# A fused graph-convolution and state-space kernel: row scaling moved behind the matmul, steps respaced over the units

## The reference, cut to what matters

```python
X = layernorm(x)
e = leaky_relu(sj[:, None, :] + si[:, :, None] + ab, 0.2)     # sj, si: X times folded vectors
alpha = adj * exp(e)
transition = alpha / (sum(alpha, -1, keepdims=True) + 1e-12)
H, Xk = 0, X
for k in range(3):
    H = H + Xk @ Wk[k] + bk[k]
    Xk = transition @ Xk
x = x + relu(H)                                               # x1
h = layernorm(x) @ W_fc1.T + b_fc1                            # then the state-space block:
u, z = split(h @ W_in.T);  u = silu(conv4(u) + conv_b)        # 1024 channels each
dt, B, C = split(u @ W_xproj.T)
delta = softplus(dt @ W_dt.T + b_dt)
s_t = exp(delta_t * A) * s_(t-1) + delta_t * u_t * B_t        # 16 states for each channel
y_t = sum over states of s_t * C_t
out = x + ((y + u * D) * silu(z)) @ W_out.T @ W_fc2.T + b_fc2
```

## Time and profile before

| | us |
|---|---|
| median of 3 runs | 4050.89 |
| lowest, highest | 4047.82, 4072.03 |
| the profiled execution | 4070.29 |
| its span, first to last instruction | 4068.2 |
| mean granted TensorE clock | 0.970 of full speed |

### The profile page before, as it was taken

How to read it: one execution, slowest core, us unless ns; L and a number is a source line. 1 busy time by engine, 2 the same in 40 slices (tenths; PEclk the granted TensorE clock), 3 DMA queues, 4 the chain that set the end, 5 groups by cost and what they waited for, 6 DMA issues and landing times. The chain is left out here.

```text
span 4068.2 us, 43314 instructions
## 1 busy us (share of the span) xinstructions
PE 3525.4 (87%) x10938; PEld 1962.4 (48%) x10938; DVE 3650.5 (90%) x3133; ACT 2835.8 (70%) x6002; POOL 3452.9 (85%) x1860
## 2 busy tenths in 40 slices
PE   6888888888888888888888888888888888888887
PEld 3544545444554444554444554444545444545443
DVE  0499999999999999999999999999999999999898
ACT  1477766777677777677777677777676777777765
POOL 0298888998888998888998888998888998888899
PEclk9889999999999999999999999999999999999999
DMA  2111101111101111101111101111101111101110
GB/s 103 49 51 54 54 11 45 51 53 53 54 8 49 51 54 53 53 9 48 51 53 53 54 7 50 51 54 53 53 11 45 51 53 53 54 11 42 47 47 8
DMA packets 50714, 183.77 MB, mean 45 GB/s; under 512 B 7339, under 2 KB 33203, under 8 KB 42067
## 3 DMA queue, kind: packets, MB, share of 16 engines
q1 hardware_dynamic: 48880, 174.17, 11.1%
q10 hardware_dynamic: 1636, 7.83, 0.5%
HBM read 164.15 MB, written 17.83 MB: 45 GB/s over the span
## 5 line engine op out<-in xcount | busy, mean ns | idle before, releaser
L408 POOL TENSOR_TENSOR st<-st,bc 128x1024 f32<-128x1024 f32 x1024 | 2400.9, 2361 | 429.1 <-DVE st L842 428.6
L842 DVE TENSOR_TENSOR_SCAN st<-dec,st 128x1024 f32<-128x1024 f32 x1024 | 2310.7, 2274 | 16.8 <-ACT dec L461 12.9
L667 PE MATMUL y_ps<-st,ident 128*128 128x512 f32 x4096 | 2010.9, 620 | 253.3 <-POOL st L408 253.3
L461 ACT ACTIVATE dec<-delta,decay 128x254 f32<-128x254 f32 x4096 | 1694.3, 467 | 612.1 <-DVE st L842 609.1
L667 PEld LDWEIGHTS y_ps<-st,ident 128*128 128x128 f32 x4096 | 770.3, 196 | 1067.8 <-issue 587.9
L830 DVE TENSOR_TENSOR st<-du,bc 128x1024 f32<-128x1024 f32 x736 | 882.1, 1199 | 5.3 <-ACT du L447 4.7
L399 POOL TENSOR_TENSOR st<-du_sb,bc 128x1024 f32<-128x1024 f32 x288 | 680.1, 2361 | 0.1
L868 DVE SCALAR_TENSOR_TENSOR u<-d_ps,chan,u 128x250 f32<-128x250 f32 (+2 forms) x768 | 307.8, 469 | 108.0 <-ACT u L501 107.3
L663 PE MATMUL y_ps<-u,diag 128*128 128x256 f32 x512 | 160.7, 441 | 229.6 <-DVE zs L849 229.6
L717 PE MATMUL d_ps<-xnT,wxz 128*128 128x256 f32 x1024 | 247.7, 385 | 6.6 <-ACT zs L510 6.6
L705 PE MATMUL d_ps<-xnT,wxz 128*128 128x256 f32 x1024 | 247.0, 384 | 6.2 <-DVE u L868 4.9
(11 more groups left out here) (99 smaller groups left out, 2527.4 us busy)
## 6 DMA issues: line engine op xcount, KB each, us to landing
bc<-bc_dram SPq DMA_DIRECT2D x64, 2048.0 KB, 10.2
xg<-x_dram SPq DMA_DIRECT2D x32, 256.0 KB, 11.5
x_dram<-xg SPq DMA_DIRECT2D x32, 256.0 KB, 2.0
last_x<-x_dram SPq DMA_DIRECT2D x32, 256.0 KB, 2.6
out_dram<-last_x SPq DMA_DIRECT2D x32, 256.0 KB, 2.2
bc<-w_inT_dram ACTq DMA_DIRECT2D x1, 4096.0 KB
adjt<-adjT_dram SPq DMA_DIRECT2D x32, 128.0 KB, 11.2
bc<-w_out_dram ACTq DMA_DIRECT2D x1, 2048.0 KB
```

What stands on the lines that cost most here:

```text
L408: nc.gpsimd.tensor_tensor(st[:, sl, :, :, :], st[:, sl, :, :, :], bc[:, p, 1, SU * q:SU * q + SU, None, :].to_broadcast([P, SU, 2, T]), AL ...
L461: a = nc.scalar.activation(dec[:, v % 2, s, j, :].rearrange("p (b t) -> p b t", b=PAIR)[:, :, 1:], delta[:, p, 2 * i + j, :].rearrange("p ...
L667: mm = nc.tensor.matmul(y_all, ident[:, :], st[:, sl, s, :, :].rearrange("p j t -> p (j t)"), start=False, stop=(q == Q - 1 and s == SU - ...
L842: nc.vector.tensor_tensor_scan(h, dec[:, v % 2, :, :, :].rearrange("p s j t -> p (s j t)"), h, 0.0, ALU.mult, ALU.add).then_inc(S["scanned ...
```

## The change

It has two parts.

First, the attention is no longer divided by its row sums before it is used. The row sum becomes two matmuls with a column of ones, which give a column per sequence (`g0[:, b:b+1]`); epsilon and reciprocal work on 128x2 (`rowsum`, `rinv`). The matmul with `att` comes first and spreads undivided values into the bank ("spread", with `x2k` in phase 18 and `x1k` in 22); ScalarE scales the two halves of the bank in place by `rinv` (phases 19 and 23); then the product with `Wk` is accumulated onto it (`hop`, phases 20 and 24, 25), without opening the bank anew.

Second, steps are respaced: u's projections to units 0, 3, 6, 9 with the taps two units behind, Silu of u 10 to 14, edge 8 to 12, Silu of z 3 to 6, the projection to dt, B, C to 15 and 16, dt to 18, 20, 22, 24, Exp to 22 and 26, Ln to 27; the graph's phases `xT` 8 to 7, third hop 9 to 8, `x2k` 11 to 9, e 12 to 10, exponentials 14 to 12, max 15 to 13, row sum 17 to 15, `x1k` 24 to 21, x1 28 to 27. z's units stay, and so do GpSimd's.

```diff
-U_STEPS = (0, 2, 4, 6)
+U_STEPS = (0, 3, 6, 9)
 Z_STEPS = (26, 27, 28, 29)
-X_STEPS = (12, 13)
-DT_STEPS = (15, 17, 19, 21)
-EXP_STEPS = (19, 23)
-LN_STEP = 24
-SILU_U, SILU_Z = 10, 3
+X_STEPS = (15, 16)
+DT_STEPS = (18, 20, 22, 24)
+EXP_STEPS = (22, 26)
+LN_STEP = 27
+SILU_U, SILU_Z = 14, 6
-FOLD_OUT = (1, 3, 5, 7)
-EDGE_STEP = 8
+FOLD_OUT = (1, 4, 7, 10)
+EDGE_STEP = 12
...
 ScalarE, graph_act
-                if v == 8:
+                if v == 7:
                     wait(act, "transposed", 2 * g + 1)
...
-                if v == 11:
+                if v == 9:
                     wait(act, "x2k_mm", g + 1)
...
-                if v == 14:
+                if v == 12:
                     wait(act, "e_mm", g + 1)
...
-                if v == 24:
+                if v in (19, 23):
+                    n = int(v == 23)
+                    wait(act, "rinv_made", g + 1)
+                    wait(act, "spread", 2 * g + 1 + n)
+                    for b in range(PAIR):
+                        half = g0[:, b * DIM:(b + 1) * DIM]
+                        a = nc.scalar.activation(half, half, ACT.Copy, scale=rinv[:, b:b + 1])
+                    a.then_inc(S["spread_scaled"], 1)
+                if v == 21:
                     wait(act, "x1k_mm", g + 1)
                     nc.scalar.activation(x1k[:, :, :].rearrange("p b d -> p (b d)"), g0[:, :], ACT.Copy)\
...
 TensorE, graph_pe
-                if v == 17:
+                if v == 15:
                     wait(pe, "alpha_made", g + 1)
-                    nc.tensor.matmul(g0[:, 0:T], ones[:, :], att[:, :, :].rearrange("p b i -> p (b i)"),
-                                     start=True, stop=True).then_inc(S["rowsum_mm"], 1)
-                if v in (21, 22):
-                    b = v - 21
-                    wait(pe, "att_made", g + 1)
-                    hop(b, 1, True, False)
-                    mm = nc.tensor.matmul(g0[:, b * DIM:(b + 1) * DIM], att[:, b, :], x2k[:, b, :],
-                                          start=False, stop=True, skip_group_check=True)
...
+                    for b in range(PAIR):
+                        mm = nc.tensor.matmul(g0[:, b:b + 1], att[:, b, :], one_col[:, 0:1], start=True, stop=True)
+                    mm.then_inc(S["rowsum_mm"], 1)
+                if v in (18, 22):
+                    if v == 18:
+                        wait(pe, "rinv_made", g + 1)
+                    else:
+                        wait(pe, "x1k_made", g + 1)
+                    for b in range(PAIR):
+                        mm = nc.tensor.matmul(g0[:, b * DIM:(b + 1) * DIM], att[:, b, :], (x2k if v == 18 else x1k)[:, b, :],
+                                              start=(b == 0), stop=False, skip_group_check=True)
+                    mm.then_inc(S["spread"], 1)
+                if v == 20:
+                    wait(pe, "spread_scaled", 2 * g + 1)
+                    for b in range(PAIR):
+                        mm = hop(b, 1, False)
+                    mm.then_inc(S["x1k_mm"], 1)
+                if v in (24, 25):
+                    b = v - 24
                     if b == 0:
-                        nc.tensor.matmul(g0[:, :], ones3, bk_row, start=True, stop=False, skip_group_check=True)
-                    hop(b, 0, False, False)
-                    mm = nc.tensor.matmul(g0[:, b * DIM:(b + 1) * DIM], att[:, b, :], x1k[:, b, :],
-                                          start=False, stop=(b == PAIR - 1), skip_group_check=True)
+                        wait(pe, "spread_scaled", 2 * g + 2)
+                        nc.tensor.matmul(g0[:, :], ones3, bk_row, start=False, stop=False, skip_group_check=True)
+                    mm = hop(b, 0, False)
...
 VectorE, conv and graph_dve
-                        if v == start + 1:
+                        if v == start + 2:
                             tap(dve, g, r, i, n)
...
-                if (v, late) == (15, 1):
+                if (v, late) == (13, 1):
                     wait(dve, "e_exp", g + 1)
...
-                if (v, late) == (19, 0):
+                if (v, late) == (16, 1):
                     wait(dve, "rowsum_mm", g + 1)
-                    nc.vector.tensor_scalar(g0[:, 0:T], g0[:, 0:T], EPS_ROW, None, ALU.add)\
+                    nc.vector.tensor_scalar(rowsum[:, :], g0[:, 0:PAIR], EPS_ROW, None, ALU.add)\
                         .then_inc(S["rowsum_eps"], 1)
                     wait(dve, "rowsum_eps", g + 1)
-                    nc.vector.reciprocal(g0[:, T:2 * T], g0[:, 0:T]).then_inc(S["rinv_made"], 1)
-                    wait(dve, "rinv_made", g + 1)
-                    nc.vector.tensor_tensor(att[:, :, :].rearrange("p b i -> p (b i)"), g0[:, T:2 * T],
-                                            att[:, :, :].rearrange("p b i -> p (b i)"), ALU.mult)\
-                        .then_inc(S["att_made"], 1)
-                if (v, late) == (28, 0):
+                    nc.vector.reciprocal(rinv[:, :], rowsum[:, :]).then_inc(S["rinv_made"], 1)
+                if (v, late) == (27, 0):
                     wait(dve, "h_mm", g + 1)
```

More of the change, by code:

```diff
@@ L124, in build @@
         x2k = sb("x2k", [P, PAIR, DIM])
-        ones = sb("ones", [P, P])
+        one_col = sb("one_col", [P, 1])
+        rinv = sb("rinv", [P, PAIR])
+        rowsum = sb("rowsum", [P, PAIR])
         last_x = sb("last_x", [P, PAIR, DIM])
@@ L176, in build @@
         dec_zeroed diag_made x_loaded adj_loaded stats aggr veps_made rstd_pow rstd_made normed transposed xT_made xnT_made
-        x2k_mm x2k_made e_mm e_exp alpha_max alpha_made rowsum_mm rowsum_eps rinv_made att_made x1k_mm x1k_made
+        x2k_mm x2k_made e_mm e_exp alpha_max alpha_made rowsum_mm rowsum_eps rinv_made spread spread_scaled x1k_mm x1k_made
         h_mm x1_made x1_stored x1_reloaded
@@ L754, in graph_pe @@
                     mm.then_inc(S["transposed"], 1)
-                if v == 9:
+                if v == 8:
                     wait(pe, "xT_made", g + 1)
                     for b in range(PAIR):
-                        mm = hop(b, 2, True, True)
+                        mm = hop(b, 2, True)
                     mm.then_inc(S["x2k_mm"], 1)
-                if v == 12:
+                if v == 10:
                     wait(pe, "x2k_made", g + 1)
@@ L771, in graph_pe @@
                     mm.then_inc(S["e_mm"], 1)
-                if v == 17:
+                if v == 15:
                     wait(pe, "alpha_made", g + 1)
-                    nc.tensor.matmul(g0[:, 0:T], ones[:, :], att[:, :, :].rearrange("p b i -> p (b i)"),
-                                     start=True, stop=True).then_inc(S["rowsum_mm"], 1)
-                if v in (21, 22):
-                    b = v - 21
-                    wait(pe, "att_made", g + 1)
-                    hop(b, 1, True, False)
-                    mm = nc.tensor.matmul(g0[:, b * DIM:(b + 1) * DIM], att[:, b, :], x2k[:, b, :],
-                                          start=False, stop=True, skip_group_check=True)
-                    if b == 1:
-                        mm.then_inc(S["x1k_mm"], 1)
@@ L786, in graph_pe @@
-                if v in (25, 26):
-                    b = v - 25
-                    wait(pe, "x1k_made", g + 1)
+                    for b in range(PAIR):
[10 more added lines that the diff above has]
+                    mm.then_inc(S["spread"], 1)
@@ L795, in graph_pe, with hop @@
                     if b == 1:
                         mm.then_inc(S["h_mm"], 1)
-            def hop(b, n, opens, closes):
+            def hop(b, n, opens):
                 for c in range(KC):
                     mm = nc.tensor.matmul(g0[:, b * DIM:(b + 1) * DIM], xT[:, c, b * L:(b + 1) * L], wks[:, n, c, :],
-                                          start=(opens and c == 0), stop=(closes and c == KC - 1),
+                                          start=(opens and c == 0), stop=(b == PAIR - 1 and c == KC - 1),
@@ L814, in _ @@
         def _(dve):
-            nc.vector.memset(ones[:, :], 1.0)
+            nc.vector.memset(one_col[:, :], 1.0)
             nc.vector.memset(ones3, 1.0)
```

## The result

The changed kernel takes 4167.48 us (median of 4 runs, 4155.02 to 4181.52) against 4053.95 of the kernel before beside it: a ratio of 1.027, 95% interval 1.0225 to 1.0322. The profiled execution took 4181.5 us, 14 us above the median.

What follows compares the result with a forecast made beforehand. VectorE, 90% busy and nearly without gaps, was taken as the bound. New waits 10.75, old waits -7.59, work -2.23, small gaps -0.4 made +0.5 us per iteration, +14 over 29: 4065 us by the median, range 3985 to 4120.

Steps and rivals of the forecast that it cites:

- VectorE's work: On VectorE, 256-column epsilon, reciprocal and multiply (2.61 us) give way to two small operations (0.38): 2.23 us saved per iteration.
- Silu's wait: Silu of u moved from unit 10 to 14, with the copy of `du`, makes scan 16 wait 1.85 us.
- Ln's: Ln moved from unit 24 to 27, behind z's first projection and bias, makes scan 29 wait 2.7 us.
- It stands in for the 1.62 at the gate of unit 18: The new 1.85 us at scan 16 replaces the old 1.62 us wait at the gate of unit 18.
- The wait at the iteration's end: `x1k`, last in ScalarE's iteration, waits for the hops: scan 0 waits 3.9 us and scan 31 0.5, plus two additions.
- loop end: ScalarE's 2.04 us standstill at the loop body's end, once in two iterations, is exposed behind `x1k`: 0.95 us per iteration.
- lower clock: TensorE, idle about 3 us before z2, runs slower, about 1.7 us in half of the iterations: 0.85 us.
- The waits that go: VectorE's old waits at taps, gate of unit 18, max and row sum could all go: 7.59 us per iteration.
- (a): Rival, chance 0.13: no new wait at scan 0, since TensorE reaches the hops before ScalarE gets to `x1k`; 3900 us.
- (b): Rival, chance 0.12: Ln is hidden in unit 27 while the other waits come; 3987 us.
- (c): Rival, chance 0.13: TensorE runs at half clock before z2 in every iteration; 4090 us.
- (d): Rival, chance 0.20: ScalarE gets stuck in units 19 to 25, scan 21 waits 1.8 us; 4117 us.

Runs made afterwards that it cites:

- the graph part alone: Attention and its hops as in the changed kernel, dense steps where the kernel before had them: 4140.87 us, 1.021 against the kernel before.

## Why the prediction was wrong

The forecast was 4065, and slower by over 1% had 0.26, for another reason. Per iteration it had +0.5; the traces say 125.9 - 122.0 = +3.9, a miss of 3.4. Added up over the same 28 iterations, VectorE's waits are 14.4 us each in the changed kernel, where 10.75 were reckoned, and 8.0 in the kernel before, where 7.59 were taken.

- **VectorE's work**: -2.23 reckoned. From the epsilon to the next inject the two small operations now take 2040.88 - 2040.63 = 0.25, so -2.36. Right (VectorE in the changed kernel):

```profile
2040.63 0.13 DVE L947 TENSOR_SCALAR rowsum<-g 128x2 f32<-128x2 f32 x1
2040.80 0.17 DVE L950 RECIPROCAL rinv<-rowsum 128x2 f32<-128x2 f32 x1
2040.88 1.22 DVE L847 TENSOR_TENSOR st<-du,bc 128x1024 f32<-128x1024 f32 x1
```

- **Silu's wait**: 1.85 at scan 16; measured 1.84. **Ln's**: 2.7 at scan 29; measured 2.72 and 2.73. Right, with their causes.
- **"It stands in for the 1.62 at the gate of unit 18"**: this is the step that failed. The gate waits 2.76 beside Silu's 1.84, not in its place; summed over the 29 rows of the timeline that stand in unit 18 it is some 78 us, 2.7 per iteration: most of the miss, by a wait that the sum had at nothing. I followed Silu through GpSimd's queue (the edge) and didn't follow what moved with it on TensorE: the two halves of the projection to dt, B, C came to stand between the sums of units 13, 14 and 15, the last of which the gate needs. The projection later by one unit took 1.8 us of that wait away, Silu and projection earlier all of it. The gate of unit 10 adds 0.6, also reckoned at nothing: in eight of the 28 iterations it waits 2.0 us. Ahead of the one at 2236 TensorE's granted clock was 0.57 from 2223 to 2235, after an idle of 2.04 us.
- **The wait at the iteration's end**: scan 31 0.5, scan 0 3.9, loop end 0.95, lower clock 0.85. In an iteration at full clock the waits were 0.55 and 3.25 + 0.35, so the mechanism and its size were right. The loop end came as reckoned: 1.1 more at inject 1 in the mean. The lower clock was undersized: in the iteration shown the z2 projection took 3.78 instead of 1.89 us and the spread behind it 1.91 instead of 1.03, 2.8 us more where I had 1.7, and z2 was that slow after 20 of its 31 idles of 2.72 us where I had taken half. It shows at scan 31, which waits 1.7 us per iteration, 3.18 in the one shown, instead of the 0.55 at full clock. In all, the end costs 1.70 at scan 31, 4.38 at inject 1 and 0.35 at scan 0, 6.4 us against 6.2 reckoned: this step is not where the forecast failed.
- **The waits that go**: taps' and max's went. But the max's wait was no cost of its own: it was Ln's, as the graph part alone shows. In the changed kernel Ln took it along to unit 27, where I had counted it, so the sum was not hurt.
- **Rivals.** (a) and (b) fell: both waits came. (c) was half right: the lower clock came in some iterations only, and cost more in each. (d) named the wrong place: in the rows of the changed kernel scan 21 doesn't wait. On the drain of 1.38 us in the Trainium skill ("ScalarE: Activation LUTs", "What ACT_TABLE_LOAD costs"): two loads and Ln again took 2048.55 - 2044.04 = 4.51 us, so none shows; the measurement decides. The lower clock came after the idle of 2.72 us before this z2 (granted clock 0.53 from 2050 to 2056), and not after the same idle in the iteration at 2433 (1.00 from 2432 to 2438; TensorE in the changed kernel):

```profile
2051.02 3.78 PE L728 MATMUL d_ps<-xnT,wxz 128*128 128x256 f32 x8 [2.72 <-ACT zs L512]
2054.60 1.91 PE L796 MATMUL g<-x2k,att 128*128 128x256 f32 x4
...
2433.45 1.99 PE L728 MATMUL d_ps<-xnT,wxz 128*128 128x256 f32 x8 [2.72 <-ACT zs L512]
```

## What to carry to other kernels

When a step is moved in a schedule of in-order queues, follow everything that must move with it on each engine, and for each find the next thing behind it that the busiest engine waits for: here a copy put last in ScalarE's iteration cost more than the reciprocal it helped to remove, and a projection between three sums made a gate wait. A wait that goes when its waiter is moved may only change its name; ask what burst made it. The parts of a change that is slower can both be good: moving its steps by one or two units turned 1.027 into 0.950.

## What the runs showed of the hardware

The same idle of TensorE, 2.72 us before the z2 projection, came 31 times in the changed kernel. After 11 of them the projection's eight passes took 1.99 us, after 20 they took 3.37 to 3.78 us; the granted clock was 1.00 in a stretch of the first kind (2432 to 2438) and 0.53 in one of the second (2050 to 2056), so most of the latter ran at 1.2 instead of 2.4 GHz. At the end of a loop body ScalarE stood still for 2.0 to 2.3 us, 13 times in the run, where the profile names no semaphore. In the kernel before, scan 0 then waited 0.36 us or not at all; in the changed kernel, where `du` is waited for, inject 1 waits 5.4 to 6.1 us in these iterations and 3.25 in nearly all others.
